# Attention with group norm on one core: the softmax in pieces of four key tiles instead of two

## What is computed

```
h      = group_norm(x)                       # 32 groups of 8 channels
q,k,v  = h @ Wq + bq, h @ Wk + bk, h @ Wv + bv
attn   = softmax(q @ k.T * 256**-0.5)        # 1024 x 1024
x_out  = x + (attn @ v) @ Wo + bo
```

## Time and profile before

| | us |
|---|---|
| median of 3 runs | 1805.01 (1804.56 to 1805.5) |
| the profiled execution | 1804.48 |
| its span, first to last instruction | 1802.8 |
| PE busy | 1796.8 (100%) |
| DVE busy | 1630.2 (90%) |
| ACT busy | 1053.5 (58%) |
| POOL busy | 91.3 (5%) |

### The profile page before, as it was taken

The page is one execution under the profiler, slowest core; times in us unless marked ns, Lnnn a source line. Parts: engine busy times, 40 slices in busy tenths (PEclk is TensorE's granted clock), DMA queues, the critical chain, the costliest instruction groups (busy, mean ns, idle before and its releaser), DMA issues.

```text
span 1802.8 us, 32710 instructions
## 1 busy us (share of the span) xinstructions
PE 1796.8 (100%) x11589; PEld 1642.5 (91%) x11589; DVE 1630.2 (90%) x2860; ACT 1053.5 (58%) x1417; POOL 91.3 (5%) x106
## 2 busy tenths in 40 slices
PE   9999999999999999999999999999999999999999
PEld 8989999899899999998999989999899898999989
DVE  7999899998998999989989999899998998999997
ACT  5565565664655656556565565565665656646563
POOL 0000000000000000000000000000000000000000
PEclk9999999999999999999999999999999999999999
DMA  3232122221222211223212222122221222311201
GB/s 117 59 71 66 21 65 58 70 70 36 45 60 68 70 47 35 70 58 70 58 23 70 58 70 61 21 69 58 70 70 32 50 60 68 70 43 39 68 14 36
DMA packets 28810, 101.92 MB, mean 57 GB/s; under 512 B 3190, under 2 KB 3963, under 8 KB 28795
## 3 DMA queue, kind: packets, MB, share of 16 engines
q0 software_dynamic: 9072, 33.03, 12.0%
q1 hardware_dynamic: 19722, 68.69, 11.7%
HBM read 68.16 MB, written 66.58 MB: 75 GB/s over the span
## 4 chain that ended last, share of the span: by engine, by line
PE 97%; DVE 2%; issue 1%; POOL 0%; ACT 0%; POOLq 0%; DVEq 0%; ACTq 0%
PE ps_s L861 48%; PE ps_o L955 13%; PE ps_o L956 13%; PE ps_o L957 13%; PE ps_o L861 10%; DVE s_buf L627 0%; PE ps_o L965 0%; DVE top L597 0%; DVE o_buf L647 0%; DVE h_lo L569 0%; DVE query_max L614 0%; POOL group_stats L298 0%; DVE bn_parts L507 0%; DVE top_turned L602 0%; DVE g_lo L577 0%
## 5 line engine op out<-in xcount | busy, mean ns | idle before, releaser
L955 PE MATMUL ps_o<-v_rows,p_hi 128*128 128x258 f32 x2048 | 577.9, 282 | 0.0
L957 PE MATMUL ps_o<-v_rows,p_lo 128*128 128x258 f32 x2048 | 576.1, 281 | 0.0
L956 PE MATMUL ps_o<-v_lo,p_hi 128*128 128x256 f32 x2048 | 575.8, 281 | 0.0
L355 ACT ACTIVATE p_hi<-s_buf 128x1024 fp32r<-128x1024 f32 x256 | 272.3, 1064 | 439.0 <-DVE s_buf L627 439.0
L861 PE MATMUL ps_s<-g_hi,h_hi 128*128 128x512 f32 x1024 | 399.4, 390 | 0.7 <-DVE g_lo L577 0.6
L861 PE MATMUL ps_s<-g_hi,h_lo 128*128 128x512 f32 x1024 | 399.0, 390 | 0.0
L861 PE MATMUL ps_s<-g_lo,h_hi 128*128 128x512 f32 x1024 | 398.6, 389 | 0.0
L955 PEld LDWEIGHTS ps_o<-v_rows,p_hi 128*128 128x128 f32 x2048 | 385.9, 188 | 2.4
L956 PEld LDWEIGHTS ps_o<-v_lo,p_hi 128*128 128x128 f32 x2048 | 384.8, 188 | 2.9
L957 PEld LDWEIGHTS ps_o<-v_rows,p_lo 128*128 128x128 f32 x2048 | 384.6, 188 | 0.0
L347 ACT ACTIVATE s_buf<-ps_s 128x512 f32<-128x512 f32 x512 | 293.0, 606 | 136.6 <-PE ps_s L861 135.3
(11 more groups left out here) (95 smaller groups left out, 2237.0 us busy)
## 6 DMA issues: line engine op xcount, KB each, us to landing
x_t<-in_x_turned_dram SPq DMA_DIRECT2D x64, 512.0 KB, 4.0
out_dram<-in_x_dram SPq DMA_DIRECT2D x63, 512.0 KB, 7.2
out_dram<-o_buf POOLq DMA_DIRECT2D x63, 512.0 KB, 5.4
x_last<-in_x_dram SPq DMA_DIRECT2D x1, 512.0 KB, 7.9
out_dram<-o_buf SPq DMA_DIRECT2D x4, 128.0 KB, 1.9
s_buf<-in_L_conv_Wq_dram SPq DMA_DIRECT2D x1, 256.0 KB, 4.8
s_buf<-in_L_conv_Wk_dram SPq DMA_DIRECT2D x1, 256.0 KB, 5.3
s_buf<-in_L_conv_Wv_dram SPq DMA_DIRECT2D x1, 256.0 KB, 5.5
```

The source lines that it names most:

```text
L355: nc.scalar.activation(p_hi[c][:, rows, :], s_buf[c][:, rows, :], ACT.Exp, scale=SCALE).then_inc(p_hi_done, 1)
L955: nc.tensor.matmul(ps[:, 0:VC], p_hi[c][:, m, cols], v_hi[:, m, :], start=m == 0, stop=False)
L956: nc.tensor.matmul(ps[:, VC - C:VC], p_hi[c][:, m, cols], v_lo[:, m, :], start=False, stop=False)
L957: last = nc.tensor.matmul(ps[:, 0:VC], p_lo[c][:, m, cols], v_hi[:, m, :], start=False, stop=m == T - 1)
```

## The change

PIECE becomes 4 and NP 2: difference, exponentials_hi, exponentials and p_rest run twice per half on 2048 columns, where they ran four times on 1024. NB = CH * NP replaces the counts of pieces in the waits, and the count of v parts that attend waits for gets a constant of its own. TensorE's work and its order stay as they are. The orders of ScalarE and VectorE are written anew.

```diff
-    PIECE = 2
+    PIECE = 4
     NP = T // PIECE
+    NB = CH * NP
+    VT = 2
...
-            def softmax_beside(b, c, project):
-
-                for i in range(NP - 1):
-                    exponentials_hi(b, c, i)
-                    if i == 1:
-                        project(2)
-                    exponentials(b, c, i)
-                    if i == 0:
-                        project(0)
-                        project(1)
-                    elif i == 1:
-                        project(3)
+            def half_softmax(b, c, project):
+                exponentials_hi(b, c, 0)
+                if c == 0:
+                    exponentials(b, c, 0)
+                for i in range(4):
+                    project(i)
+                if c == 1:
+                    exponentials(b, c, 0)
+            def scores_beside(b, c, eb, ec):
+
+                scores_out(b, c, 0)
+                exponentials_hi(eb, ec, 1)
+                scores_out(b, c, 1)
+                exponentials(eb, ec, 1)
+                for m in range(2, T):
+                    scores_out(b, c, m)
...
             def body(b):
 
-                softmax_beside(b, 0, lambda i: v_part(b, i))
+                half_softmax(b, 0, lambda i: v_part(b, i))
                 scores_out(b, 1, 0)
-                last_exponentials(b, 0)
-                for m in range(1, T - 1):
+                exponentials_hi(b, 0, 1)
+                scores_out(b, 1, 1)
+                exponentials(b, 0, 1)
+                for m in range(2, T - 1):
                     scores_out(b, 1, m)
                 shift(b + 1, 0)
                 scores_out(b, 1, T - 1)
                 shift(b + 1, 1)
                 h_parts(b + 1)
-                softmax_beside(b, 1, lambda i: g_part(b + 1, i))
+                half_softmax(b, 1, lambda i: g_part(b + 1, i))
...
                 difference(b, c, 0)
-                difference(b, c, 1)
                 finish_tile(2)
-                difference(b, c, 2)
+                if c == 0:
+                    difference(b, c, 1)
                 next_stats()
                 project(0)
                 next_sums()
                 finish_tile(3)
                 project(1)
+                if c == 1:
+                    difference(b, c, 1)
+                project(2)
+                project(3)
                 p_rest(b, c, 0)
-                project(2)
-                difference(b, c, 3)
-                project(3)
                 p_rest(b, c, 1)
-                p_rest(b, c, 2)
-                p_rest(b, c, 3)
```

More of the change, by code:

```diff
@@ L343, in scores_out @@
             def scores_out(b, c, m):
-                after(act, p_lo_done, b * 8 + (4 * c + m // PIECE + 1 - 8))
+                after(act, p_lo_done, b * NB + (NP * c + m // PIECE + 1 - NB))
                 act.wait_ge(s_ps, b * 16 + (8 * c + m + 1))
@@ L421, in first_image @@
                 scores_out(0, 1, 2)
+                scores_out(0, 1, 3)
                 exponentials(0, 0, 1)
[L423 to L426, removed]
                 for m in range(4, T - 1):
@@ L436, in first_image @@
                 g_part(1, 2)
+                g_part(1, 3)
                 exponentials(0, 1, 0)
[L438 to L457, removed]
+                scores_beside(1, 0, 0, 1)
             def body(b):
-                softmax_beside(b, 0, lambda i: v_part(b, i))
+                half_softmax(b, 0, lambda i: v_part(b, i))
                 scores_out(b, 1, 0)
-                last_exponentials(b, 0)
-                for m in range(1, T - 1):
+                exponentials_hi(b, 0, 1)
+                scores_out(b, 1, 1)
+                exponentials(b, 0, 1)
+                for m in range(2, T - 1):
                     scores_out(b, 1, m)
@@ L469, in body @@
                 h_parts(b + 1)
-                softmax_beside(b, 1, lambda i: g_part(b + 1, i))
+                half_softmax(b, 1, lambda i: g_part(b + 1, i))
             def last_image(b):
[L474 to L477, removed]
+                scores_beside(b, 0, b - 1, 1)
                 scores_out(b, 1, 0)
@@ L494, in _ @@
             with act.Fori(2, B - 1) as b:
-                scores_first(b)
+                scores_beside(b, 0, b - 1, 1)
                 body(b)
@@ L713, in first_image @@
                 v_rest(0, FIRST_V[0], 0)
+                v_rest(0, FIRST_V[1], 1)
                 difference(0, 0, 1)
[L715 to L719, removed]
                 v_rest(0, FIRST_V[2], 2)
                 v_rest(0, FIRST_V[3], 3)
-                p_rest(0, 0, 2)
-                p_rest(0, 0, 3)
+                p_rest(0, 0, 0)
+                p_rest(0, 0, 1)
                 for step in range(5):
@@ L735, in first_image @@
                 g_rest(1, 1)
-                difference(0, 1, 1)
                 g_rest(1, 2)
                 g_rest(1, 3)
-                difference(0, 1, 2)
+                difference(0, 1, 1)
+                finish(0, 0, 2)
                 p_rest(0, 1, 0)
-                difference(0, 1, 3)
-                finish(0, 0, 2)
+                finish(0, 0, 3)
+                maxima(1, 0, 0)
                 p_rest(0, 1, 1)
[L744 to L747, removed]
                 for step in range(1, 5):
@@ L809, in last_image @@
                 difference(b, 0, 1)
-                difference(b, 0, 2)
+                maxima(b, 1, 0)
                 p_rest(b, 0, 0)
-                difference(b, 0, 3)
+                maxima(b, 1, 1)
                 p_rest(b, 0, 1)
[L814 to L817, removed]
                 for step in range(2, 5):
@@ L829, in last_image @@
                 difference(b, 1, 0)
+                finish(b, 0, 0)
                 difference(b, 1, 1)
-                finish(b, 0, 0)
-                difference(b, 1, 2)
+                finish(b, 0, 1)
                 p_rest(b, 1, 0)
-                difference(b, 1, 3)
-                finish(b, 0, 1)
+                finish(b, 0, 2)
                 p_rest(b, 1, 1)
-                p_rest(b, 1, 2)
-                finish(b, 0, 2)
-                p_rest(b, 1, 3)
                 finish(b, 0, 3)
@@ L951, in attend @@
                     if j == 0 and m % PIECE == 0:
-                        pe.wait_ge(p_lo_done, b * 8 + (4 * c + m // PIECE + 1))
-                        if by_piece:
-                            pe.wait_ge(v_lo_done, b * 4 + (m // PIECE + 1))
+                        pe.wait_ge(p_lo_done, b * NB + (NP * c + m // PIECE + 1))
+                    if j == 0 and by_piece and m % VT == 0:
+                        pe.wait_ge(v_lo_done, b * 4 + (m // VT + 1))
                     nc.tensor.matmul(ps[:, 0:VC], p_hi[c][:, m, cols], v_hi[:, m, :], start=m == 0, stop=False)
```

10 lines of the change are left out of this document (4 added, 6 removed).

## The result

The changed kernel takes 1928.3 us against 1804.8 of the kernel before on the same chip: 1.068 times as long, 95% interval 1.067 to 1.069. The forecast was 1888.6 with a range of 1868 to 1908: slower as forecast, but 39.7 us too little, and outside the range.

> The changed kernel once more, for a trace of an undisturbed execution. Median about 1928.3 us. It is 40 us above the forecast of 1888.6. Theory clock: the stop of TensorE is the one forecast, 2.3 to 2.6 us ahead of scores(b+1,0,0), and the rest is TensorE at its lower clock behind it: part of the stages after the stop has matmuls of 512 columns more than 0.23 us apart, mean granted clock 0.987, some 1.4 us per image.

A forecast was written before the change was run, and what follows sets the result against it. TensorE was taken to bound the kernel before, with a chain over ScalarE and VectorE stopping it afterwards. 29 images at 2.62 us (76.0), plus 5.8 and 2.3, make 84.1 on 1804.5: 1888.6 us, range 1868 to 1908.

The forecast's parts named there:

- The sum: Adds 76.0 us for 29 images, 5.8 for images 0 and 1, 2.3 for the last: 84.1 on top of 1804.5.
- the chain's links: Queue steps from scores(b,1) to the first matmul of scores(b+1,0): TensorE goes on at 30.28 instead of 27.79, waiting 2.49 us.
- What bounds the kernel, and what takes over: TensorE sets the time before; afterwards a chain over ScalarE and VectorE makes it wait for g's low parts, 2.49 us per image.
- Size of the instructions: One instruction of 2048 columns takes 2.28 us on VectorE and 1.95 on ScalarE, at the upper end 2.10.
- Of these 0.10 was a wait for the copy of tile 5 ... 4.75: shift starts at 13.29: Link from the last p_rest's end to shift(b+1,0): 4.85 us before, 4.75 without the wait for tile 5's copy.
- POOL's power ... has VectorE's two maxima beside it as before: GpSimd's power for the variance, before turn_back, keeps the same VectorE neighbours; no cost was counted.
- TensorE's restart: End of the chain: g_rest(b+1,1) starts at 29.50 and is done at 30.24; TensorE may go on at 30.28.
- A second wait ... 0.13: At tile 2 of scores(b+1,0), TensorE waits 0.13 us for g's third part, which stands behind the whole of difference(b,1,1).
- The clock falls ... 7%: Rival, 7%: TensorE's clock drops to 1.2 GHz behind each stop; with 3 us, 45 us on top, 1934.
- Images 0, 1 and the last: Extra time at the run's ends: 5.8 us (1 to 8) for images 0 and 1, 2.3 (1 to 4) for the last.
- The saved fixed cost: Rival, 5%: fewer, larger instructions save overhead on VectorE and ScalarE, so not slower: 1804 to 1805 us or some 1 less.

The follow-up runs named there:

- g_first: The changed kernel, but in half B ScalarE copies g parts 0 and 1 ahead of the first exponential; 1845.68 us.
- exp_early: The changed kernel, but half A's third exponential runs ahead of the copies of v, the fourth right behind the copy of tile 0; 1849.85 us.
- split: The changed kernel's order, but each instruction of 2048 columns is two of 1024 in a row, each with its own semaphore count; 1858.53 us.
- power_alone: The kernel awake, with VectorE's turn_back moved right behind group_variance, so VectorE stands idle during GpSimd's power; 1912.11 us.
- awake: The changed kernel, with ten spare matmuls of 512 columns on TensorE ahead of its wait for the low parts of g; 1906.99 us.
- reordered: The edits of g_first and exp_early, plus v parts 0 and 1 copied ahead of half A's third exponential and the last image's tile 3 copied first; 1812.48 us.
- awake_five: As awake, but with five spare matmuls in TensorE's stop instead of ten; 1907.52 us.
- both: The changed kernel with the edits of g_first and exp_early together, pieces of 2048 columns kept; 1831.42 us.

## Why the forecast was right in kind and too small

Two steps failed. The sum had nothing for the clock, which cost some 20 us, and the chain's links were taken too short, which cost some 18. In detail:

- **What bounds the kernel, and what takes over: right.** TensorE's stop for the low parts of g, in 31 places, ends on the chain that was written down, link for link. g_first, exp_early and split each shorten one part of that chain and each shortens the stop.
- **Size of the instructions: right.** 2.286 against 2.28. The exponential is 0.04 shorter than taken (1.914 against 1.95), which the short gaps about it use up again. The Trainium skill ("ScalarE: Activation LUTs", What ACT_TABLE_LOAD costs) gives 186 ns + 0.833 ns a column for an instruction whose scale and bias are immediate values, an estimate of 1892 ns for 2048; the measured 1914 lies between this and the forecast.
- **"Of these 0.10 was a wait for the copy of tile 5 ... 4.75: shift starts at 13.29": wrong.** The link is 5.10. This wait was taken away as a plain saving, and it was not: it had let GpSimd's power start ahead of VectorE's maxima. Without it the maxima go first, the power takes 2.05 us instead of 1.03, and VectorE then waits for it: 0.35 us more in each image. The sentence "POOL's power ... has VectorE's two maxima beside it as before" had the company right and missed who comes first. That the neighbour is the cause is shown by power_alone; that it came first, by the timelines above.
- **TensorE's restart: too small.** 0.87 us from the start of the last g_rest to the first matmul, where 0.78 was taken (0.09), and 0.07 between the difference and the exponential. With the 0.35, less 0.05 elsewhere, the stop is 2.95 instead of 2.49, from start to start.
- **"A second wait ... 0.13": 0.27.** scores(b+1,0) takes 11.16 us instead of 10.89. Most of it is no idle time: the first matmul holds 0.33 us instead of 0.23, and so does the first of tile 2 (1026.36 to 1026.69), which starts 0.13 us after g_rest 2 is done. The sum had neither 0.10. Together: 3.22 an image instead of 2.62, and 29 x 0.60 = 17.4 us.
- **"The clock falls ... 7%": it did, in part.** The size of one fall was right (1.47 us against the 1.5 of the rival), its number not: 13 of 29 turns, where the rival had all 30 and the forecast none. The row used against it, a clock of 1.00 behind the end of TensorE's work, was a weak one, 1.8 us long, and a run has nothing after it. awake gives 20.4 us in all, 19.4 of them in images 2 to 30 and 1.0 in the last. What decides in which image the clock falls is not shown: the stops of the images that kept it are as long (2.78 against 2.79).
- **Images 0, 1 and the last: 5.8 + 2.3 forecast, 7.5 + 3.5 measured.** Without the 1.2 us ahead of the first scores and the clock's 1.0 in the last image it is 6.4 + 2.5, so these terms were nearly right. The last image loses its part where the forecast put it. ScalarE's copy of tile 3 (before) and TensorE's wait for it:

```profile
1880.14 0.58 ACT L349 ACTIVATE s_buf<-ps_s 128x512 f32<-128x512 f32 x1
```

```profile
1880.77 0.50 PE L827 MATMUL ps_s<-g_hi,h_hi 128*128 128x512 f32 x1 [0.99 <-ACT s_buf L349]
```

- Together: 17.4 + 19.1 + 1.7 + 1.2 = 39.4 of the 39.7 us. By awake, some 20 of it is the clock, the rival that had 7%; 1.2 lie ahead of the first scores; the rest, some 18, is the forecast's own mechanism with links that were sized too small.
- **The saved fixed cost: real and worth nothing.** VectorE works 13.8 us less and ScalarE 19.4, and none of it reaches the end, not even in reordered, where TensorE alone sets the image.

## What to carry to other kernels

When instructions are merged, ask of every short instruction behind them who waits for it, and give the larger pieces an order of their own: the same pieces cost 123 us in one order and 7.5 in another. Once a forecast contains a stop of TensorE of nearly 3 us in every round, the lower clock belongs into it as a likely case, priced per stop, not into a small rival. And a short wait that a change removes may be what keeps two engines in a good order: before it is counted as a gain, look at who starts next to it within 0.1 us.

## What the runs showed of the hardware

- The granted clock behind a stop of TensorE. Stops of 2.79 us were followed by some 3 us at 0.50 in 13 of 29 images; stops of 1.66 us (awake_five) and of 1.26 us (split), about thirty each, by none. The single stop of 2.71 us ahead of scores(31,0) in awake and in awake_five, and that of 2.83 in power_alone, were followed by none either. A single stop of 2.06 us in the last image of g_first was followed by the first line below, and one of 2.81 in the last image of both by the second:

```profile
1798.70:1799.70 1.00, 1.00 (x4) 0.71 (x4) 0.35 (x2) 1.00 (x2) 0.00 (x0) 0.50 0.00 0
...
1782.50:1788.00 5.50, 5.50 (x21) 4.92 (x21) 4.29 (x3) 5.50 (x5) 0.00 (x0) 0.50 0.01 3
```

- The same 128x4 power on GpSimd takes 1.03 us or 2.05, and what decides is whether VectorE's instruction with two inputs starts 0.03 us after it or 0.07 us ahead of it (no run puts an instruction with one input there). VectorE's own instruction beside it is not longer in either case (1.23 us).
- A matmul of 512 columns behind a stop is shown with 0.49 us and the next follows 0.33 after its start, where 0.39 and 0.23 are usual: every stop costs 0.10 us beyond its wait.
